# Moving two transposes of gate rows and two outputs in the hand-written order of a gated attention and feed-forward block

## The chip, the cores and the metric

The kernel runs on one core of a Trainium2 chip. The metric is the device time of one execution in microseconds (us); lower is better. TensorE does the matrix products and the transposes, VectorE (DVE in the rows) and ScalarE (ACT) read its results out of PSUM, GpSimd (POOL) does masks and a few elementwise operations, and SyncE (SP) issues all DMA transfers.

## The reference, cut to what matters

A batch of 16 sequences of 256 tokens, 512 wide, goes through two gated blocks:

```python
x = x + tanh(g_xattn[0]) * xattn(layernorm(x), ctx, ctx, ...)
x = x + tanh(g_ffn[0]) * ffn(layernorm(x), w_gate, w_up, w_down)
```

`xattn` has 8 heads of width 64. For each head two gates come from a product of the concatenated inputs with small matrices. With `cs` the running sum of `log_sigmoid(fg)` over the tokens and `a = ig - cs`, the decay matrix is `D = exp(cs_i + a_j - max_log_D_i)` for `j <= i`, so its row maximum is a running maximum of `a` along the tokens. The head is `(q k^T / 8 * D) / normaliser @ v`, followed by a root-mean-square norm of each head.

`ffn` quantises its input to 8 bits per token and its weights to {-1, 0, 1}. It computes `g = x @ w_gate.T` and `u = x @ w_up.T` (2048 wide), then `h = relu(g)**2 * u`, quantises `h` with the maximum of `|h|` in the token's row, and multiplies with `w_down.T` back to 512.

## The kernel before

The sequences are worked off one after another, each as two tiles `t = 0, 1` of 128 tokens. There are 16 steps. Step `b` (`par` is its parity) interleaves three sequences: the feed-forward block of `b`, the attention of `n = b + 1`, and the gates of `m = b + 2`. In the last two steps `m` is None, and in the last one `n` is None too. Each engine has its own list of work, written out by hand in a function `step`, and works it off strictly in order; semaphores join the lists. What an engine waits for therefore holds up all that stands behind it in its own list.

A feed-forward tile is four chunks of 512 hidden columns. `chunk(b, t, c)` on TensorE is four matmuls with the gate weights into the PSUM bank `gb[c % 2]` and four with the up weights into `ub[c % 2]` (L1090). ScalarE takes the relu of `gb` (L524) and squares it (L526). VectorE multiplies with `ub` in `hidden(b, t, c)` (L755); that product also frees the `ub` bank for chunk `c + 2`. `hidden_max` finds the row maximum in two parts: part 0 over three chunks (L762) and part 1 over the fourth (L767). `hidden_scale` (L777 to L782) makes the scale from it, and `quantise_low` on VectorE (L788) with `quantise_high` on ScalarE (L544) quantise half of the row each. `hidden_transposes` (L1104, 16 of them) turns the quantised rows, `hidden_cols` copies them out of PSUM (ScalarE L538, VectorE L796), `down` is 16 matmuls into the one bank `yb` (L1116), and `output(b, t)` on VectorE (L805) scales the bank, adds the residual and so frees it for the next `down`. SyncE stores the result.

The attention of `n`: `scores` (L1124, L1125) fills the banks `ab`, `weigh` on VectorE (L862) multiplies them with the decay matrix, which ScalarE's `exponentials` (L564, L570) and GpSimd's `masks` (L429) have made, and `heads_out` (L1137) multiplies with the values. Then `normaliser`, `head_squares`, `scale_heads` (L896, L900), `residual` (VectorE L908 for tile 0, GpSimd L436 for tile 1), `token_stats` (L915, L919), `token_centres`, `quantise_tokens`, `token_columns` (L1198).

The gates of `m`: `cumulative_sum` on TensorE (L1174, L1175), `cumulative` on VectorE (L842 copies the sums, L843 makes `a`), `a_rows` on TensorE (L1180, two transposes of `a`), `running_max` on VectorE (L848, a scan of these rows), `max_columns` on TensorE (L1187). SyncE's `spread_max` carries the rows through DRAM into the decay matrix.

All of the gates' small products share the PSUM bank `tp`, and the wait in front of `a_rows` is that `a` has been made:

```python
pe.wait_ge(tp_free, gate_use(m, CUMSUM) + 1)
```

GpSimd's `residual` waits for VectorE's last `output` as well (`gp.wait_ge(o_ready, 2 * n - 2)`), since `x2` of that parity is still being read by it.

Of the kernel before, what the change touches and what calls it, by code (L numbers as in the profile page):

```python
# [32 lines left out]
def gated_block(nc, x, ctx_t, ctx_v, small_in, w_gate, w_up, w_down, max_rows, out):  # L33
# [12 lines left out]
    KF = FF // P  # L46
# [7 lines left out]
    with ExitStack() as stack:  # L54
# [669 lines left out]
        def _(dve):  # L724
# [25 lines left out]
            def hidden(b, t, c):  # L750

                k = 8 * b + 4 * t + c
                dve.wait_ge(r2_ready, k + 1)
                dve.wait_ge(u_full, k + 1)
                nc.vector.tensor_tensor(h[t][:, c * CH:(c + 1) * CH], relu[:, c % 2, :], ub[c % 2][:, :],  # L755
                                        ALU.mult).then_inc(h_done, 1)
# [28 lines left out]
            def quantise_low(b, t):  # L785

                dve.wait_ge(quant_step, QUANT_K * (2 * b + t) + 5)
                nc.vector.tensor_scalar(hq[t][:, 0:FF // 2], h[t][:, 0:FF // 2], hqs[:, t:t + 1], MAGIC16,  # L788
                                        ALU.mult, ALU.add).then_inc(quant_step, 1)
# [9 lines left out]
            def output(b, t, xpar):  # L799
                k = 2 * b + t  # L800
                dve.wait_ge(y_full, k + 1)
                dve.wait_ge(dq_ready, k + 1)
                if not at(b, 0):
                    dve.wait_ge(out_done[t], 16 * b)
                nc.vector.scalar_tensor_tensor(ot[t][:, :], yb[:, :], dq[:, t:t + 1], x2[xpar][:, t, :],  # L805
                                               ALU.mult, ALU.add).then_inc(o_ready, 1)
# [32 lines left out]
            def cumulative(m, par):  # L839
                dve.wait_ge(tp_full, FULL * (gate_use(m, CUMSUM) + 1))  # L840
                cs = tp[:, 0:T * NH].rearrange("p (t g) -> p t g", t=T)
                nc.vector.tensor_copy(csum[:, :, :], cs).then_inc(gate_step, 1)  # L842
                nc.vector.tensor_tensor(a[par][:, :, :], gates[:, :, 0:NH], cs, ALU.subtract).then_inc(tp_free, 1)  # L843

            def running_max(m, par):

                dve.wait_ge(tp_full, FULL * (gate_use(m, A_ROWS) + 1))
                nc.vector.tensor_tensor_scan(mrow[:, :], tp[0:NH, 0:S], zeros8[:, :], LOWEST,  # L848
                                             ALU.max, ALU.add).then_inc(tp_free, 1)
# [44 lines left out]
            def scale_heads(n):  # L894
                dve.wait_ge(rms_step, 2 * n + 2)
                nc.vector.scalar_tensor_tensor(scl[:, :, :], rz[:, :, :], tanhs[:, 0:1], rn[:, :, :],  # L896
                                               ALU.mult, ALU.mult).then_inc(post_step, 1)
                dve.wait_ge(post_step, POST_K * n + 9)
                for t in range(T):
                    nc.vector.tensor_tensor(yo[:, t, :].rearrange("p (h d) -> p h d", d=HD), ysb[:, t, :, 0:HD],  # L900
                                            scl[:, t, :, None].to_broadcast([P, NH, HD]), ALU.mult).then_inc(post_step, 1)
# [89 lines left out]
            def step(b, n, m, par):  # L991
                npar = 1 - par
                prev = not at(b, 0)
                if n is not None:
                    weigh(n, 0)
                    weigh(n, 1)
                hidden(b, 0, 0)
                if m is not None:
                    attention_stats(m, par)
                if n is not None:  # L1000
                    weigh(n, 2)
                    weigh(n, 3)
                hidden(b, 0, 1)
                if n is not None:
                    weigh(n, 4)
                    weigh(n, 5)
                hidden(b, 0, 2)
                if n is not None:
                    weigh(n, 6)
                    weigh(n, 7)  # L1010
                if m is not None:
                    attention_norm(m, par)
                hidden_max(b, 0, 0)
                hidden(b, 0, 3)
                if prev:
                    hidden_cols(b - 1, 1)
                hidden_max(b, 0, 1)
                if n is not None:
                    normaliser(n, npar)
                if not prev:  # L1020
                    weight_scale(2)
                    dve.wait_ge(winv_step, WINV[2])
                    nc.vector.scalar_tensor_tensor(wprod[:, 2:3], wmean[:, 2:3], 1.0 / 127.0, tanhs[:, 1:2],
                                                   ALU.mult, ALU.mult).then_inc(winv_step, 1)
                hidden_scale(b, 0, par)
                quantise_low(b, 0)
                if n is not None:
                    head_squares(n)
                if m is not None:
                    gates_in(m)  # L1030
                if n is not None:
                    mean_squares(n)
                if m is not None:
                    log_forget(m)
                if n is not None:
                    scale_heads(n)
                if prev:
                    output(b - 1, 1, npar)
                if m is not None:
                    cumulative(m, par)  # L1040
                if n is not None:
                    residual(n, npar)
                if m is not None:
                    running_max(m, par)
                if n is not None:
                    token_stats(n, npar)
                hidden(b, 1, 0)
                if n is not None:
                    token_centres(n, npar)
                hidden(b, 1, 1)  # L1050
                if n is not None:
                    quantise_tokens(n)
                hidden_cols(b, 0)
                hidden(b, 1, 2)
                if m is not None:
                    negated_max(m)
                hidden_max(b, 1, 0)
                hidden(b, 1, 3)
                hidden_max(b, 1, 1)
                output(b, 0, par)  # L1060
                hidden_scale(b, 1, par)
                quantise_low(b, 1)

            schedule(dve, step)
            hidden_cols(LAST, 1)
# [4 lines left out]
        def _(pe):  # L1070
# [172 lines left out]
            def step(b, n, m, par):  # L1243
                npar = 1 - par
                prev = not at(b, 0)
                chunk(b, 0, 0, par)
                if n is not None:
                    scores(n, 0, npar)
                    scores(n, 1, npar)
                chunk(b, 0, 1, par)  # L1250
                if n is not None:
                    scores(n, 2, npar)
                    scores(n, 3, npar)
                    heads_out(n, 0, npar)
                chunk(b, 0, 2, par)
                if n is not None:
                    scores(n, 4, npar)
                    scores(n, 5, npar)
                    heads_out(n, 1, npar)
                    scores(n, 6, npar)  # L1260
                    scores(n, 7, npar)
                chunk(b, 0, 3, par)
                if n is not None:
                    heads_out(n, 2, npar)
                if prev:
                    hidden_transposes(b - 1, 1)
                else:
                    weight_total(2)
                if n is not None:
                    heads_out(n, 3, npar)  # L1270
                if m is not None:
                    q_columns(m, par)
                if prev:
                    down(b - 1, 1, 0, KF // 2)
                if m is not None:
                    gate_products(m, par, 0, 2 * T * KD)
                if prev:
                    down(b - 1, 1, KF // 2, KF)
                if m is not None:
                    cumulative_sum(m)  # L1280
                chunk(b, 1, 0, par, 0, 1)
                if m is not None:
                    a_rows(m, par)
                chunk(b, 1, 0, par, 1, 2)
                chunk(b, 1, 1, par)
                hidden_transposes(b, 0)
                chunk(b, 1, 2, par)
                if m is not None:
                    max_columns(m)
                down(b, 0, 0, KF // 2)  # L1290
                chunk(b, 1, 3, par)
                if n is not None:
                    token_columns(n)
                down(b, 0, KF // 2, KF)

            schedule(pe, step)
            hidden_transposes(LAST, 1)
# [34 lines left out]
```

## Time and profile before

| | |
|---|---|
| time, median of 3 runs | 637.5 us (636.77 to 637.85) |
| profiled execution, its own time | 638.38 us |
| profiled execution, span of the instructions | 636.7 us |
| TensorE matmul busy | 578.6 us, 91% of the span |
| VectorE busy | 526.7 us, 83% |
| ScalarE busy | 454.3 us, 71% |
| GpSimd busy | 129.9 us, 20% |
| mean granted TensorE clock | 0.965 |

The span runs from the first to the last instruction; the execution's own time lies 1.7 us above it. The first 100 us or so prepare the weights, and step 0 is mixed with that; from then on a step is repeated every 35.2 us. Timeline rows give the start in us from the start of the span, the time from the first start to the last end of the group, engine, source line and operation, what is written from what, and the number of instructions; a bracket is the idle time of the engine ahead of it and the instruction that is taken to have ended it.

### The profile page before, as it was taken

The page shows a single profiled execution, that of the slowest core. Times are in us where ns is not written, and L with a number is a line of the kernel's source. Part 1 is how long each engine was busy: PE and PEld are TensorE (multiplying, and loading weights), DVE is VectorE, ACT ScalarE, POOL GpSimd, SP SyncE. Part 2 cuts the span into 40 slices and gives each one's busy share as a digit, 9 for nine tenths or more (in the row PEclk, how much of TensorE's full clock was granted, in tenths as well). Part 3 has the DMA queues.
Part 4 walks back from the last instruction along what each step waited for, and adds up shares of the span by engine and source line. Part 5 has one row for each costly group of instructions (what it writes and reads, how often), then busy time and mean ns, then how long its engine had stood idle before and what let it go on. Part 6 is the DMA issues. An engine that isn't in the chain of part 4 may idle for free.

```text
span 636.7 us, 18420 instructions
## 1 busy us (share of the span) xinstructions
PE 578.6 (91%) x6596; PEld 338.0 (53%) x6596; DVE 526.7 (83%) x1144; ACT 454.3 (71%) x925; POOL 129.9 (20%) x266
## 2 busy tenths in 40 slices
PE   7592768999999999999999999999999999999896
PEld 4361443656555564656555565646565555656442
DVE  4479595898989989898989899898989899897964
ACT  5374979858685877858686868768586868677662
POOL 1256240212121202112121202021121212021200
PEclk9785968999999999999999999999999999999998
DMA  9884505041140505050320505050412305020000
GB/s 311 306 287 139 192 2 167 18 140 62 43 159 17 182 0 199 0 182 17 103 95 19 179 8 191 0 187 11 156 43 77 121 17 183 3 100 1 34 19 33
DMA packets 45169, 63.73 MB, mean 100 GB/s; under 512 B 1872, under 2 KB 26704, under 8 KB 45136
## 3 DMA queue, kind: packets, MB, share of 16 engines
q1 hardware_dynamic: 45136, 63.30, 28.8%
q8 instruction: 20, 0.33, 0.2%
q14 instruction: 13, 0.11, 0.1%
HBM read 54.77 MB, written 8.52 MB: 99 GB/s over the span
## 4 chain that ended last, share of the span: by engine, by line
PE 59%; DVE 17%; issue 10%; ACT 6%; DMA 5%; DVEq 1%; POOL 1%; SPq 0%; ACTq 0%; POOLq 0%
PE ub L1090 15%; PE gb L1090 14%; PE yb L1116 10%; PE ab L1124 6%; PE tp L1137 5%; PE ab L1104 3%; DVE ssq L883 3%; DMA stage<-in_w_up 2%; PE ab L1125 2%; DVE stage L805 2%; DMA xs<-in_x 2%; DVE stage L755 1%; DMA max_rows<-mrow 1%; PE ab L1198 1%; DVE dmat L862 1%
## 5 line engine op out<-in xcount | busy, mean ns | idle before, releaser
L1090 PE MATMUL ub<-wuT,xqT 128*128 128x512 bf16 x512 | 133.1, 383 | 2.0 <-DVE stage L755 2.0
L1090 PE MATMUL gb<-wgT,xqT 128*128 128x512 bf16 x512 | 133.3, 383 | 1.5 <-ACT xqT L551 1.5
L524 ACT ACTIVATE relu<-gb 128x512 f32<-128x512 f32 x128 | 75.4, 589 | 77.3 <-PE gb L1090 75.1
L1116 PE MATMUL yb<-wdT,stage 128*128 128x512 bf16 x512 | 122.8, 384 | 3.6 <-ACT stage L538 3.6
L755 DVE TENSOR_TENSOR stage<-relu,ub 128x512 f32<-128x512 f32 x128 | 87.0, 680 | 26.6 <-ACT relu L526 26.1
L862 DVE SCALAR_TENSOR_TENSOR dmat<-ab,dmat 128x384 f32<-128x384 f32 x128 | 65.3, 551 | 31.7 <-POOL dmat L429 22.7
L526 ACT ACTIVATE relu<-relu 128x512 f32<-128x512 f32 x128 | 80.7, 631 | 4.1
L1090 PEld LDWEIGHTS ub<-wuT,xqT 128*128 128x128 bf16 x512 | 50.3, 99 | 61.2 <-DVE stage L755 3.0
L1116 PEld LDWEIGHTS yb<-wdT,stage 128*128 128x128 bf16 x512 | 47.4, 99 | 53.4 <-issue 4.7
L1090 PEld LDWEIGHTS gb<-wgT,xqT 128*128 128x128 bf16 x512 | 46.0, 100 | 49.9 <-ACT xqT L551 1.8
L429 POOL TENSOR_SCALAR_AFFINE_SELECT dmat<-dmat 128x256 f32<-128x256 f32 x128 | 55.3, 461 | 68.0 <-ACT dmat L570 67.9
L1137 PE MATMUL tp<-values,dmat 128*64 128x65 f32 x1536 | 60.4, 229 | 3.6 <-issue 3.6
L1137 PEld LDWEIGHTS tp<-values,dmat 128*64 128x64 f32 x1536 | 51.5, 141 | 15.9 <-issue 10.8
L1124 PE MATMUL ab<-qT,cT 64*128 64x256 f32 x256 | 52.7, 437 | 5.4 <-DVE dmat L862 5.4
L570 ACT ACTIVATE dmat<-dmat,a 128x256 f32<-128x256 f32 x128 | 57.3, 496 | 0.0
L762 DVE TENSOR_REDUCE stage<-stage 128x1 f32<-128x1536 f32 x32 | 56.0, 1749 | 0.1
L459 POOL TENSOR_SCALAR dq<-hm,wprod 128x1 f32<-128x1 f32 x32 | 9.1, 284 | 222.8 <-DVE rhm L780 217.7
L564 ACT ACTIVATE dmat<-dmat,a 128x128 f32<-128x128 f32 x128 | 43.7, 391 | 7.0 <-DMA dmat<-max_rows 7.0
L436 POOL TENSOR_TENSOR x<-ysq,xs 128x512 f32<-128x512 f32 x16 | 28.4, 1774 | 82.4 <-DVE stage L805 78.3
L544 ACT ACTIVATE hq<-stage,hqs 128x1024 f16<-128x1024 f32 x32 | 36.7, 1146 | 5.7 <-DVE hqs L782 5.7
L578 ACT ACTIVATE ysb<-tp 128x260 f32<-128x260 f32 x64 | 24.5, 382 | 22.5 <-PE tp L1137 22.5
L1124 PEld LDWEIGHTS ab<-qT,cT 64*128 64x128 f32 x256 | 24.8, 188 | 26.5 <-issue 19.3
(110 smaller groups left out, 870.8 us busy)
## 6 DMA issues: line engine op xcount, KB each, us to landing
dmat<-max_rows SPq DMA_DIRECT2D x16, 1024.0 KB, 5.1
values<-in_ctx_v SPq DMA_DIRECT2D x16, 520.0 KB, 7.7
xs<-in_x SPq DMA_DIRECT2D x16, 512.0 KB, 5.9
cT<-in_ctx_t SPq DMA_DIRECT2D x16, 512.0 KB, 6.9
out<-stage SPq DMA_DIRECT2D x32, 256.0 KB, 2.0
stage<-in_w_gate SPq DMA_DIRECT2D x4, 1024.0 KB, 12.7
stage<-in_w_up SPq DMA_DIRECT2D x4, 1024.0 KB, 11.1
stage<-in_w_down SPq DMA_DIRECT2D x4, 1024.0 KB, 5.6
```

The lines of the kernel that those rows point to most:

```text
L429: nc.gpsimd.affine_select(out=dv, in_=dv, compare_op=ALU.is_ge, fill=0.0, base=0, pattern=[[0, 2], [1, P]], channel_multiplier=-1).then_in ...
L524: nc.scalar.activation(relu[:, c % 2, :], gb[c % 2][:, :], ACT.Relu).then_inc(g_free, 1)
L526: nc.scalar.activation(relu[:, c % 2, :], relu[:, c % 2, :], ACT.Square).then_inc(r2_ready, 1)
L564: nc.scalar.activation(dmat[:, hd, 2, :], dmat[:, hd, 1, :], ACT.Exp, bias=a[npar][:, 1, hd:hd + 1], scale=-1.0).then_inc(e_low, 1)
L570: last = nc.scalar.activation(dh, dh, ACT.Exp, bias=a[npar][:, 0, hd:hd + 1], scale=-1.0)
L755: nc.vector.tensor_tensor(h[t][:, c * CH:(c + 1) * CH], relu[:, c % 2, :], ub[c % 2][:, :], ALU.mult).then_inc(h_done, 1)
L762: nc.vector.tensor_reduce(h[t][:, FF:FF + 1], h[t][:, 0:3 * CH], axis=AX_X, op=ALU.max, apply_absolute_value=True).then_inc(quant_step, 1)
L862: nc.vector.scalar_tensor_tensor(dh, ab[hd % 2][:, 0:3 * P], HD ** -0.5, dh, ALU.mult, ALU.mult).then_inc(a_free[hd % 2], 1)
L1090: last = nc.tensor.matmul(bank[c % 2][:, :], xqT[par][:, t, d, :], w[:, d, c * CH:(c + 1) * CH], start=(d == 0), stop=(d == KD - 1))
L1116: done = nc.tensor.matmul(yb[:, :], hqT[:, c, :], wdT[:, c, :], start=(c == 0), stop=(c == KF - 1))
L1124: nc.tensor.matmul(ab[e][:, 0:S], cT[npar][rows, kd, 0:P], qT[npar][rows, kd, 0:S], start=True, stop=True)
L1137: done = nc.tensor.matmul(tp[rows, (2 * t + e) * VW:(2 * t + e + 1) * VW], dmat[:, hd, block, rows], values[npar][:, s, hd, :], start=firs ...
```

## The change

In every step that has an `m`, TensorE's `a_rows` goes from the middle of `chunk(b, 1, 0)` (between its gate half and its up half) to behind the whole chunk, and VectorE's `cumulative` goes ahead of `output(b - 1, 1)`. In the last two steps (no `m`), VectorE's `hidden(b, 1, 0)` goes ahead of `token_stats`. In the last step (no `n`), TensorE takes `chunk(b, 1, 3)` ahead of the whole of `down(b, 0)`, which was split around it, and VectorE's `output(b, 0)` goes behind `hidden_scale` and `quantise_low` of tile 1. No instruction is added or removed.

```diff
@@ VectorE, step
                     scale_heads(n)
+                if m is not None:
+                    cumulative(m, par)
                 if prev:
                     output(b - 1, 1, npar)
-                if m is not None:
-                    cumulative(m, par)
                 if n is not None:
                     residual(n, npar)
                 if m is not None:
                     running_max(m, par)
+                else:
+                    hidden(b, 1, 0)
                 if n is not None:
                     token_stats(n, npar)
-                hidden(b, 1, 0)
+                if m is not None:
+                    hidden(b, 1, 0)
...
                 hidden_max(b, 1, 1)
-                output(b, 0, par)
+                if n is not None:
+                    output(b, 0, par)
                 hidden_scale(b, 1, par)
                 quantise_low(b, 1)
+                if n is None:
+                    output(b, 0, par)
@@ TensorE, step
-                chunk(b, 1, 0, par, 0, 1)
+                chunk(b, 1, 0, par)
                 if m is not None:
                     a_rows(m, par)
-                chunk(b, 1, 0, par, 1, 2)
                 chunk(b, 1, 1, par)
                 hidden_transposes(b, 0)
                 chunk(b, 1, 2, par)
                 if m is not None:
                     max_columns(m)
-                down(b, 0, 0, KF // 2)
-                chunk(b, 1, 3, par)
-                if n is not None:
+                if n is not None:
+                    down(b, 0, 0, KF // 2)
+                    chunk(b, 1, 3, par)
                     token_columns(n)
-                down(b, 0, KF // 2, KF)
+                    down(b, 0, KF // 2, KF)
+                else:
+                    chunk(b, 1, 3, par)
+                    down(b, 0, 0, KF)
```

## Rows read from the trace of the kernel before

**Rows 1.** Busy time of each engine in one step, from the windows.

```profile
290.10:325.30 35.20, 34.18 (x409) 20.24 (x408) 31.14 (x71) 26.06 (x58) 6.62 (x15) 1.00 0.26 90
```

**Rows 2.** Waits of TensorE: total us, times, longest.

```profile
PE tp L1180 <- DVE a L843: 12.1, 14, 0.9
```

**Rows 3.** Timeline of TensorE in that step, where the gates' rows are transposed.

```profile
308.44 1.02 PE L1090 MATMUL gb<-wgT,xqT 128*128 128x512 bf16 x4
310.38 0.38 PE L1180 MATMUL tp<-ident,a 128*8 128x128 f32 x2 [0.92 <-DVE a L843]
...
314.94 1.03 PE L1090 MATMUL ub<-wuT,xqT 128*128 128x512 bf16 x4
```

**Rows 4.** Timeline of VectorE beside it.

```profile
309.42 0.75 DVE L805 SCALAR_TENSOR_TENSOR stage<-yb,dq,x 128x512 f32<-128x512 f32 x1
...
310.24 0.68 DVE L908 TENSOR_TENSOR x<-ysq,xs 128x512 f32<-128x512 f32 x1
310.84 0.67 DVE L848 TENSOR_TENSOR_SCAN mrow<-tp,zeros 8x256 f32<-8x256 f32 x1
...
313.04 0.69 DVE L755 TENSOR_TENSOR stage<-relu,ub 128x512 f32<-128x512 f32 x1
```

**Rows 5.** Timeline of GpSimd's residual, in that step and two before the end.

```profile
310.25 1.81 POOL L436 TENSOR_TENSOR x<-ysq,xs 128x512 f32<-128x512 f32 x1 [5.54 <-DVE stage L805]
...
590.91 0.68 DVE L908 TENSOR_TENSOR x<-ysq,xs 128x512 f32<-128x512 f32 x1
...
591.15 1.57 POOL L436 TENSOR_TENSOR x<-ysq,xs 128x512 f32<-128x512 f32 x1 [5.37 <-DVE stage L805]
```

**Rows 6.** Timeline of TensorE and VectorE in the next step, scores and weighing.

```profile
324.11 0.40 PE L1125 MATMUL ab<-qT,cT 64*128 64x128 f32 x4
...
324.62 1.02 DVE L862 SCALAR_TENSOR_TENSOR dmat<-ab,dmat 128x384 f32<-128x384 f32 x2 [0.32 <-POOL dmat L429]
...
327.13 0.92 PE L1137 MATMUL tp<-values,dmat 128*64 128x65 f32 x24
...
330.85 1.02 DVE L862 SCALAR_TENSOR_TENSOR dmat<-ab,dmat 128x384 f32<-128x384 f32 x2 [1.53 <-POOL dmat L429]
...
332.78 1.04 PE L1090 MATMUL gb<-wgT,xqT 128*128 128x512 bf16 x4
```

**Rows 7.** Timeline of the last step but one (b = 14), TensorE and ScalarE.

```profile
594.25 1.01 ACT L538 ACTIVATE stage<-ab 128x1024 bf16<-128x1024 f16 x1
...
594.45 1.04 PE L1090 MATMUL ub<-wuT,xqT 128*128 128x512 bf16 x4 [1.82 <-DVE stage L755]
595.40 1.89 PE L1116 MATMUL yb<-wdT,stage 128*128 128x512 bf16 x8
```

**Rows 8.** Timeline of the last step (b = 15), TensorE.

```profile
619.33 1.89 PE L1116 MATMUL yb<-wdT,stage 128*128 128x512 bf16 x8
...
626.89 1.71 PE L1104 MATMUL ab<-identh,hq 128*128 128x128 f16 x16 [2.22 <-DVE hq L788]
629.02 4.35 PE L1116 MATMUL yb<-wdT,stage 128*128 128x512 bf16 x16 [0.41 <-ACT stage L538]
```

**Rows 9.** Timeline of the last step, VectorE.

```profile
620.68 1.75 DVE L762 TENSOR_REDUCE stage<-stage 128x1 f32<-128x1536 f32 x1
623.41 0.69 DVE L755 TENSOR_TENSOR stage<-relu,ub 128x512 f32<-128x512 f32 x1 [0.98 <-ACT relu L526]
624.14 0.69 DVE L767 TENSOR_REDUCE hmax<-stage 128x1 f32<-128x513 f32 x1
...
625.40 0.20 DVE L777 TENSOR_SCALAR hm<-hmax,c 128x1 f32<-128x1 f32 x1
```

**Rows 10.** Timeline of TensorE's same work earlier in the last step.

```profile
607.93 1.06 PE L1104 MATMUL ab<-identh,hq 128*128 128x128 f16 x16
609.81 3.61 PE L1116 MATMUL yb<-wdT,stage 128*128 128x512 bf16 x16 [0.82 <-ACT stage L538]
```

**Rows 11.** Window of TensorE near the end: busy us, granted clock, DMA share, GB/s.

```profile
626.80:628.80 2.00, 1.71 (x16) 0.58 0.12 44
```

## The prediction

> **What bounds the kernel now.** I first read the windows of one step, to see which engine has no room. In 35.2 us TensorE is busy for 34.18, VectorE for 31.14, ScalarE for 26.06 and GpSimd for 6.62 [rows 1]. So a step costs what TensorE's list costs, plus its own waits. The waits of TensorE come next: one kind repeats, `a_rows` waiting for `a` from VectorE, 12.1 us in 14 waits of at most 0.9 [rows 2]. The timeline shows its place. TensorE starts the gate half of `chunk(b, 1, 0)` at 308.44 and stands for 0.92 us until 310.38 [rows 3]. VectorE is then in `output(b - 1, 1)`, at 309.42; the two small instructions of `cumulative` sit between it and `residual` at 310.24 [rows 4]. Behind the wait stand four up matmuls that need nothing of it. The last view was the timeline of the last two steps, where no `a_rows` exists, and where the end of the kernel is a chain through VectorE and not TensorE's work [rows 8, 9].
>
> **Part 1: `a_rows` behind the chunk, `cumulative` ahead of the output.** A group of four matmuls takes 0.86 us of TensorE's time: 16 take 3.61 and 8 take 1.89, so eight more cost 1.72 [rows 8, 10]. With both halves of the chunk ahead of it, TensorE comes to `a_rows` at 308.44 + 2 x 0.86 = 310.16, some 0.1 later with the change of operands. `cumulative` now starts where the output did, at 309.42, and its two instructions are short: rows that follow each other on VectorE overlap by some 0.08 (310.24 + 0.68 against 310.84), so the output takes 0.67 of the 0.82 us up to `residual`, and the two together 0.15. So `a` is there by about 309.7. There is 0.5 us to spare and the wait goes. The whole of it is TensorE's time: everything behind starts 0.92 earlier.
>
> What VectorE gives for it: `output` comes 0.16 later and `residual` still starts at 310.24. `running_max` starts at 310.84 [rows 4]; the transposes, started at about 310.26 and 0.38 long [rows 3], end at 310.64, a little earlier than now. So the scan, SyncE's transfer of the rows behind it and `max_columns` stay where they are. The output frees `yb` for `down(b, 0)` four groups later, and its store is not waited for here. Both are free.
>
> GpSimd's residual waits for that output. It starts at 310.25 and ends at 312.06; in step 14 it takes 1.57 and not 1.81, and in both cases it ends 1.13 or 1.14 us behind the end of VectorE's own residual (310.92; 591.59 against 592.72) [rows 4, 5]. I take from this that its end hangs on VectorE's residual, which does not move: 0 us. The other bound is that it slips by the output's 0.16. That pushes `token_stats` and `hidden(b, 1, 0)` by as much, and it is this product that frees the bank for the up half of chunk 2: it ends at 313.73, TensorE will want it at 314.94 - 0.92 = 314.02 [rows 3, 4]. Even 0.16 later it is in time. The Trainium skill, SBUF — State Buffer, section "Who interferes with whom", says that a VectorE instruction with two SBUF inputs and a GpSimd instruction that reads SBUF exclude each other for the length of an instruction; by it the slip is 0, by the start of the output alone it would be 0.16 a step, and neither changes the time of TensorE here by more than 0.1 a step.
>
> **Is there room for a shorter step in the other engines?** TensorE now leads VectorE by 0.92 more from `a_rows` until VectorE next waits for it. VectorE idles in the next step for 1.53 and 0.32 in front of `weigh` [rows 6]. The critical hand-off is `weigh(1)`: the scores of heads 2 and 3 need its bank. The pattern is seen at `weigh(4)`, `weigh(5)`, which end at 331.87 while the chunk behind the next pair of scores starts at 332.78, so 0.91 later [rows 6]. `weigh(1)` ends at 325.64, so `heads_out(0)` can't start before 326.55, and TensorE wants it at 327.13 - 0.92 = 326.21 [rows 6]. If `weigh(0)` stays at 324.62, 0.34 of each 0.92 is lost. Its row names GpSimd's mask for the 0.32 idle, but the last scores of heads 0 and 1 start at 324.11 and end at 324.51, just ahead of it, and these come 0.92 earlier. The same releaser is named at 330.85, behind a mask that belongs to a later pair. So I hold it for a wait on TensorE: `weigh(0)` moves up by 0.32 to 324.30, `weigh(1)` ends at 325.32, and the bound on `heads_out(0)` is 326.23 against the wanted 326.21. The two loops are as good as equal, and I take the full gain; the bounds are 0.58 and 0.92 a step.
>
> The wait is counted 14 times, but in step 0, with the weights still being made, it is next to nothing, and 13 steps carry it at 0.92: **12.0 us**. The bounds are 13 x 0.58 = 7.5 and 13 x 0.98 = 12.7 (if 0.06 of the hand-off goes too).
>
> **Part 2: the product ahead of the token statistics.** In step 14 TensorE waits 1.82 us for `hidden(14, 1, 0)` in front of the up half of chunk 2, at 594.45 [rows 7]. With the product some 2 us earlier this wait goes, but what is behind it is `down`, at 595.40. It needs ScalarE's copy, which starts at 594.25 and ends at 595.26 [rows 7]; the one in the last step ends 0.15 ahead of its `down` too. In front of this copy ScalarE's list has the logarithm for the token statistics, and these wait for GpSimd's residual, until 592.72 [rows 5], whatever stands ahead of them. So the stall only moves from the up half to `down`, as a pause of 1.82 + 0.2 = about 2.0: **0 us**. Its other bound is the whole 1.82 of gain, if the copy is early, which its order on ScalarE excludes. VectorE is 0.6 us (one product) further on; TensorE has no wait on it until the end, so this too is 0. In the last step the edit moves nothing, since there `token_stats` is absent.
>
> **Part 3: the last step.** Now eight matmuls of `down` start at 619.33, ahead of chunk 3 [rows 8]. They go behind, so chunk 3 comes 1.72 earlier and its product is no longer late: it is bound by the large maximum in front of it, 620.68 + 1.67 = 622.35, and not by 623.41 [rows 9]. That is 1.06. Behind it stand the small maximum at 624.14 and, after the output, the scale at 625.40 [rows 9]. Without the output the scale can start when the maximum is done, 624.14 + 0.69 + 0.07 = 624.90, which gives 0.50. The sum is **1.56 us** on the chain to the last transposes at 626.89. The 16 matmuls of `down(15, 0)` end about 619.33 + 1.72 + 3.45 = 624.5, ahead of the transposes at 625.33. The output, moved behind the quantiser, ends about 626.0; the last `down` needs it and the transposes' copy, which is there at 627.3. So it is covered by 1.3 us. Bounds: 1.06 and 1.72 + 0.66 = 2.38.
>
> **The clock.** At 626.89, after TensorE had stood 2.22 us, the transposes take 1.71 and run at a granted clock of 0.58, with parts at 1.2 GHz; the last `down` takes 4.35 [rows 8, 11]. The same two groups at 607.93 and 609.81 take 1.06 and 3.61, behind pauses of at most 0.82 [rows 10]. From the first transpose to `down` it is 2.13 us now and was 1.88 there. At the full clock the tail is shorter by 0.25 + 0.74 = 0.99. The pause ahead of the transposes shrinks from 2.22 to about 0.8, the size of the one that did no harm, so I take **0.99 us**; bounds 0 and 0.99.
>
> **The sum.** 12.0 + 0 + 1.56 + 0.99 = 14.6 us. Against the profiled execution's own time of 638.38 (a span of 636.7 with 1.7 around it) this gives 623.8. The median of the runs, 637.5, is 0.9 lower, and whether it has the slow clock at its end is not known. Taken from it, the time would be 622.9. I forecast **623.0 us**. The likeliest case's own range is 621.8 to 624.6.
>
> **Rivals.**
> (A) VectorE's loop becomes the bound: `weigh(0)` really waits for GpSimd's mask, or the hand-off is tighter than read. Then a step gains 0.58: 7.5 + 2.6 = 10.1, and 627.4 us. For it speaks the releaser in the row; against it the end of the scores just ahead.
> (B) The clock falls elsewhere. In step 14 the pause grows to 2.0, between 1.82 (no fall) and 2.22 (a fall) [rows 7, 8]. A low stretch costs, by the two groups above, up to 0.65 + 0.74 = 1.4 us: 624.4. With the last clock low as well, 625.4.
> (C) The wait only moves: after `a_rows` comes earlier relative to VectorE, TensorE meets a later wait of the same size in each step, and only the end gains, 2.6: 634.9. For it speaks VectorE's 31.14 busy of 35.2; against it, that its idle time ahead of `weigh` alone is 1.85 a step, twice the gain.
> (D) Slower. The rows reach the scan late. VectorE stands in front of `running_max` and all of its list behind is late, up to `weigh` of the next step. There are 0.2 us of room before it starts. To undo the 0.92 and the end's 2.6 the rows must come about 0.2 + 0.34 + 0.92 = 1.5 us later than I have them; at 2 us later, 13 x 0.5 - 2.6 gives about 641 us. The rows' timeline leaves no such lateness.
>
> **How the numbers follow.** The sum as it stands 0.73, A 0.12, B 0.08, C 0.04, D 0.03. A measurement here can tell about 0.2%, 1.3 us. All cases but D are faster than that, and something for what I have not thought of goes to the same and the slower side: faster 0.94, same 0.02, slower 0.04. The range reaches from all upper bounds together, 637.5 - 12.7 - 2.38 - 0.99 = 621.4, up to A: 621.5 to 627.5.
>
> **What the profile of the changed kernel would show.** In every step, `a_rows` without idle time in front and `running_max` in its old place behind VectorE's residual; steps 34.3 us apart; `hidden(b, 1, 0)` ending just ahead of the up half of chunk 2; VectorE's idle time in front of `weigh` down to some 0.6 in place of 1.53, and none at `weigh(0)`. In step 14, no wait at the up half but about 2.0 at `down`, on ScalarE's copy. In the last step, a pause of about 0.8 ahead of the transposes, which take 1.06, and a last `down` of 3.61. The forecast is wrong if TensorE waits in front of the scores of heads 2 and 3 or of chunk 2 in each step, or if the steps stay above 34.7 us.

## The result and the profile after

The changed kernel takes 620.49 us (median of 4, 619.63 to 621.43) against 637.15 us for the kernel before (median of 4 runs on the same chip). The ratio is 0.9738, with a 95% interval from 0.972 to 0.9755: 2.6% faster. The forecast was 623.0 with a range from 621.5 to 627.5, so the sign was right and the gain, 16.7 us where the sum had 14.6, was larger than the range allowed. The profiled execution has a span of 619.7 us, where it was 636.7: 17.0 us less.

The timeline of TensorE in the changed kernel, at the place that answers to [rows 3]:

```profile
302.56 1.02 PE L1096 MATMUL gb<-wgT,xqT 128*128 128x512 bf16 x4
303.42 1.03 PE L1096 MATMUL ub<-wuT,xqT 128*128 128x512 bf16 x4
304.28 0.38 PE L1186 MATMUL tp<-ident,a 128*8 128x128 f32 x2
304.50 1.03 PE L1096 MATMUL gb<-wgT,xqT 128*128 128x512 bf16 x4
```

No bracket stands in front of the rows (L1186). The distance from start to start tells more: from the gate half of chunk 0 to that of chunk 1 it is 304.50 - 302.56 = 1.94 us. Before, the gate half started at 308.44 and the rows at 310.38 [rows 3]; the rows hold TensorE for 0.22 and the up half for 0.86, so the next chunk began 3.02 behind the first:

```profile
310.60 1.03 PE L1090 MATMUL ub<-wuT,xqT 128*128 128x512 bf16 x4
311.46 1.03 PE L1090 MATMUL gb<-wgT,xqT 128*128 128x512 bf16 x4
```

The difference is 1.08 us, and not the 0.92 of the bracket. The rows of VectorE that answer to [rows 4, 5], and GpSimd's:

```profile
303.54 0.17 DVE L842 COPY csum<-tp 128x16 f32<-128x16 f32 x1
303.63 0.16 DVE L843 TENSOR_TENSOR a<-gates,tp 128x16 f32<-128x16 f32 x1
303.70 0.74 DVE L805 SCALAR_TENSOR_TENSOR stage<-yb,dq,x 128x512 f32<-128x512 f32 x1
304.37 0.68 DVE L908 TENSOR_TENSOR x<-ysq,xs 128x512 f32<-128x512 f32 x1
304.97 0.67 DVE L848 TENSOR_TENSOR_SCAN mrow<-tp,zeros 8x256 f32<-8x256 f32 x1
...
304.53 1.65 POOL L436 TENSOR_TENSOR x<-ysq,xs 128x512 f32<-128x512 f32 x1 [5.70 <-DVE stage L805]
...
318.21 1.00 DVE L862 SCALAR_TENSOR_TENSOR dmat<-ab,dmat 128x384 f32<-128x384 f32 x2
...
323.90 1.02 DVE L862 SCALAR_TENSOR_TENSOR dmat<-ab,dmat 128x384 f32<-128x384 f32 x2 [1.00 <-POOL dmat L429]
```

The scan stands where it did, 0.60 behind the start of VectorE's residual. GpSimd's residual starts 0.15 later after VectorE's than it did, and is shorter by as much: it ends at 306.18, which is 1.13 behind the end of VectorE's own (305.05); in the two rows of before it was 1.14 and 1.13. `weigh(0)` at 318.21 has no idle time in front of it any more.

The last two steps, TensorE, answering to [rows 7, 8]:

```profile
578.08 1.03 PE L1096 MATMUL ub<-wuT,xqT 128*128 128x512 bf16 x4
581.03 1.89 PE L1122 MATMUL yb<-wdT,stage 128*128 128x512 bf16 x8 [1.92 <-ACT stage L538]
...
606.90 3.40 PE L1122 MATMUL yb<-wdT,stage 128*128 128x512 bf16 x15
610.92 1.07 PE L1110 MATMUL ab<-identh,hq 128*128 128x128 f16 x16 [0.62 <-DVE hq L788]
612.80 3.61 PE L1122 MATMUL yb<-wdT,stage 128*128 128x512 bf16 x16 [0.82 <-ACT stage L538]
```

The wait of step 14 is now in front of `down`, as forecast. In the last step the pause ahead of the transposes is 0.62, they take 1.07 and the last `down` 3.61, at the full clock.

**Where the 17.0 us came from.** I set the start of the rows in each step against that of before. In steps 3 to 13 the distance from one step to the next fell from 35.22 to 34.16, 1.06 each, 11.7 us in 11 steps. Step 2 fell from 35.95 to 34.18: 1.06 again, and 0.7 us that only the kernel before had, a pause in the middle of its gate products. Steps 0 and 1 together have 0.9, mixed with what the preparation of the weights shifted (this allows for the up half that now stands ahead of the rows), step 14 has nothing, and the last step gives 2.6. In sum 11.7 + 1.8 + 0.9 + 2.6 = 17.0.

### The profile page after: what moved, and what is told of

Its sections match the earlier page's. It is cut to its first block, busy times and chain, and to the rows that moved or that the text cites. A ratio compares the mean times of both kernels' runs of the same rounds, so it can differ in the third digit from the quotient of the medians.

```text
span 619.7 us, 18325 instructions
## 1 busy us (share of the span) xinstructions
PE 565.0 (91%) x6517; PEld 337.9 (55%) x6596; DVE 524.0 (85%) x1144; ACT 454.4 (73%) x925; POOL 127.9 (21%) x266
## 4 chain that ended last, share of the span: by engine, by line
PE 75%; ACT 7%; DVE 7%; DMA 5%; issue 5%; SPq 1%; POOL 0%; DVEq 0%; ACTq 0%
PE yb L1122 17%; PE gb L1096 16%; PE ub L1096 16%; PE tp L1143 7%; PE ab L1130 6%; PE ab L1110 4%; PE tp L1170 3%; DMA stage<-in_w_up 2%; PE ab L1153 2%; PE ab L1131 2%; DMA max_rows<-mrow 2%; PE ab L1204 1%; DMA xs<-in_x 1%; ACT wdT L516 1%; ACT wdT L506 1%
## 5 line engine op out<-in xcount | busy, mean ns | idle before, releaser
L1096 PE MATMUL gb<-wgT,xqT 128*128 128x512 bf16 x480 | 128.1, 385 | 6.0 <-issue 4.0
L1096 PE MATMUL ub<-wuT,xqT 128*128 128x512 bf16 x498 | 130.2, 383 | 0.8
L1122 PE MATMUL yb<-wdT,stage 128*128 128x512 bf16 x482 | 114.3, 379 | 8.0 <-ACT stage L538 4.9
L436 POOL TENSOR_TENSOR x<-ysq,xs 128x512 f32<-128x512 f32 x16 | 26.3, 1644 | 83.7 <-DVE stage L805 79.6
L1130 PEld LDWEIGHTS ab<-qT,cT 64*128 64x128 f32 x256 | 25.3, 190 | 25.7 <-issue 16.7
```

The source lines that it names most:

```text
L1096: last = nc.tensor.matmul(bank[c % 2][:, :], xqT[par][:, t, d, :], w[:, d, c * CH:(c + 1) * CH], start=(d == 0), stop=(d == KD - 1))
L1122: done = nc.tensor.matmul(yb[:, :], hqT[:, c, :], wdT[:, c, :], start=(c == 0), stop=(c == KF - 1))
L1130: nc.tensor.matmul(ab[e][:, 0:S], cT[npar][rows, kd, 0:P], qT[npar][rows, kd, 0:S], start=True, stop=True)
```

## The experiments

Theory S: the bracket shows less than the wait costs. It is counted from the modelled end of the last matmul (309.46), while the next one could have begun at 308.44 + 0.86 = 309.30 [rows 3]. Theory B: the bracket is all of it, and the rest of the gain came from elsewhere. The first four runs shared a chip; the kernel before took 636.84 there (13 runs).

**Part 1 alone (e1).** Only the two moves for the rows, as in the diff of the change.

```diff
+                if m is not None:
+                    cumulative(m, par)
                 if prev:
                     output(b - 1, 1, npar)
-                if m is not None:
-                    cumulative(m, par)
...
-                chunk(b, 1, 0, par, 0, 1)
+                chunk(b, 1, 0, par)
                 if m is not None:
                     a_rows(m, par)
-                chunk(b, 1, 0, par, 1, 2)
```

> Part 1 alone (rows behind the chunk, cumulative ahead of the output). Theory S: the wait in front of the rows was worth 1.08 us of TensorE's time a step, not the 0.92 that stood in the bracket, because the matmul ahead of it gives its place free 0.16 before its modelled end. Then 13 steps give 13.8 to 14.0 and the time is 623.2 (622.5 if the 0.7 in step 2 goes as well). Theory B: the bracket was the whole wait, and the rest of the gain of 2 us came from elsewhere, a code fetch or the clock: 12.0, so 625.2.

Measured: 623.27 us, ratio 0.9783 (0.9746 to 0.982), steps 34.14 to 34.19 us apart. S holds: it is the steps that tell, since a gain from elsewhere would not stand in each of them, and they are 1.06 us shorter than the 35.22 of before. Its last `down`, still in the old order, takes 5.03 us.

**Part 3 alone (e2).** Only the order of the last step.

```diff
-                down(b, 0, 0, KF // 2)
-                chunk(b, 1, 3, par)
-                if n is not None:
+                if n is not None:
+                    down(b, 0, 0, KF // 2)
+                    chunk(b, 1, 3, par)
                     token_columns(n)
-                down(b, 0, KF // 2, KF)
+                    down(b, 0, KF // 2, KF)
+                else:
+                    chunk(b, 1, 3, par)
+                    down(b, 0, 0, KF)
...
-                output(b, 0, par)
+                if n is not None:
+                    output(b, 0, par)
                 hidden_scale(b, 1, par)
                 quantise_low(b, 1)
+                if n is None:
+                    output(b, 0, par)
```

> Part 3 alone, only the last step's order. Both theories: 1.56 us less chain on VectorE, and with no low clock at the end 0.99 more, so 634.6; without the clock's share 635.6. Theory S has no say on step 2: if the 0.7 us in the gate products of step 2 are a code fetch that depends on where the step falls in time, they are still there, as in the kernel before.

Measured: 634.74 us, ratio 0.996 (0.9943 to 0.9976), steps 35.22 apart, the last `down` at 3.61 us. Its size is as expected. The pause of the kernel before in step 2 is absent here (168.58 - 133.36 = 35.22), though the steps are those of the kernel before, so it is not the change that takes it away.

**Rows moved, sums not (e3).** TensorE's edit alone.

```diff
-                chunk(b, 1, 0, par, 0, 1)
+                chunk(b, 1, 0, par)
                 if m is not None:
                     a_rows(m, par)
-                chunk(b, 1, 0, par, 1, 2)
```

> Only a_rows behind the whole chunk, cumulative still behind the output. The result a is ready at the same moment as in the kernel before, 310.32, and TensorE's place is free at 310.17, while the modelled end of the matmuls is 310.33. Theory S: 0.21 us are still lost a step although the trace will show a bracket of 0.05 or none; gain 0.86 a step, 626.0, that is 2.6 more than with both halves. Theory B: with no idle time in the bracket nothing is lost, so within 0.6 us of the run with both halves.

Measured: 627.95 us, ratio 0.9853 (0.9818 to 0.9887), 4.7 us more than with both halves (e1), steps 34.36 apart. This is the run that decides. Its timeline of TensorE:

```profile
304.21 1.02 PE L1090 MATMUL gb<-wgT,xqT 128*128 128x512 bf16 x4
305.07 1.03 PE L1090 MATMUL ub<-wuT,xqT 128*128 128x512 bf16 x4
306.16 0.38 PE L1180 MATMUL tp<-ident,a 128*8 128x128 f32 x2
306.38 1.03 PE L1090 MATMUL gb<-wgT,xqT 128*128 128x512 bf16 x4
```

No bracket, and yet the next chunk starts 2.17 us behind the first and not 1.94. The 0.23 us are lost with no bracket in TensorE's list: the rows begin 1.09 behind the up half, where 0.86 is enough. That they wait for `a` stands in the rows of the weight load (PEld), which takes `a` into TensorE ahead of the transpose:

```profile
305.94 0.16 DVE L843 TENSOR_TENSOR a<-gates,tp 128x16 f32<-128x16 f32 x1
306.15 0.09 PEld L1180 LDWEIGHTS tp<-ident,a 128*8 128x8 f32 x2 [0.56 <-DVE a L843]
```

`a` is done at 306.10, the load begins at 306.15 and the transposes at 306.16, which is only 0.06 behind the modelled end of the up half (305.07 + 1.03). From step to step it is 34.36 against 34.16, so of the 4.7 us 13 x 0.20 = 2.6 is this. The rest is not in the steps. The profile of e3 has the pause in step 2 again (0.7 us), which e1's has not, and its last `down` takes 6.48 us at half the clock, 1.45 more than e1's.

```profile
615.79 1.10 PE L1104 MATMUL ab<-identh,hq 128*128 128x128 f16 x16 [2.22 <-DVE hq L788]
617.67 6.48 PE L1116 MATMUL yb<-wdT,stage 128*128 128x512 bf16 x16 [0.78 <-ACT stage L538]
```

```profile
616.70:623.50 6.80, 6.02 (x17) 0.50 0.00 0
```

The second fence is the window of TensorE over that stretch: the granted clock is 0.50.

**Sums moved, rows not (e4).** VectorE's edit alone.

```diff
+                if m is not None:
+                    cumulative(m, par)
                 if prev:
                     output(b - 1, 1, npar)
-                if m is not None:
-                    cumulative(m, par)
```

> Only cumulative ahead of the output, a_rows still between the halves of the chunk. The result a is ready at 309.66, 0.66 earlier than before. Both theories: the bracket falls from 0.92 to 0.26 and each step gains 0.66, so 628.6. If the position of the rows in TensorE's list were the cause alone, there would be no gain: 637.2.

Measured: 630.03 us, ratio 0.9882 (0.9847 to 0.9917), steps 34.57 apart, so 0.65 a step. The bracket reads as expected. Set against the changed kernel it speaks for S too: the bracket is 0.26, but the rows begin 1.29 behind the gate half, where 0.86 is enough, and the steps are 0.41 longer than 34.16. The profile shows one thing that can account for the 1.4 us over the expectation: its last `down` takes 6.47 us, where the kernel before had 4.35.

```profile
304.61 1.02 PE L1090 MATMUL gb<-wgT,xqT 128*128 128x512 bf16 x4
305.90 0.38 PE L1180 MATMUL tp<-ident,a 128*8 128x128 f32 x2 [0.26 <-DVE a L843]
```

**Part 2 alone (e5).** The next four runs shared a chip as well; the kernel before took 637.15 there.

```diff
                 if m is not None:
                     running_max(m, par)
+                else:
+                    hidden(b, 1, 0)
                 if n is not None:
                     token_stats(n, npar)
-                hidden(b, 1, 0)
+                if m is not None:
+                    hidden(b, 1, 0)
```

> Part 2 alone, the product ahead of the token statistics in the last two steps, in the kernel before. My theory: the 1.82 us of wait in step 14 only move from the up half of chunk 2 to the down product behind it, which waits for ScalarE's copy: about 2.0 there, gain 0, so the time of the kernel before. Rival: the wait was VectorE's and is gained, 1.8 us.

Measured: 637.71 us, ratio 1.0007 (0.9991 to 1.0023). By the medians the three parts alone take 13.6, 2.1 and -0.6 us off, 15.1 in sum, and the whole change 16.7; e1's interval alone is 2.3 us wide to either side, so no interaction of the parts can be read from that. The wait stands in front of `down`:

```profile
595.67 1.89 PE L1119 MATMUL yb<-wdT,stage 128*128 128x512 bf16 x8 [1.91 <-ACT stage L538]
```

This run also has the old order at its end, and there the clock did not fall, although the pause is the same 2.22 us as before:

```profile
627.16 1.07 PE L1107 MATMUL ab<-identh,hq 128*128 128x128 f16 x16 [2.22 <-DVE hq L788]
629.05 3.61 PE L1119 MATMUL yb<-wdT,stage 128*128 128x512 bf16 x16 [0.82 <-ACT stage L538]
```

**ScalarE's copy first (e6).** Made on the changed kernel; `hidden(b, 1, 0)` also goes ahead of `token_stats` in every step.

```diff
-                if n is not None:
-                    tokens_rstd(n)
                 hidden_cols(b, 0)
+                if n is not None:
+                    tokens_rstd(n)
```

> The changed kernel, with ScalarE's copy for the down product ahead of its logarithm for the token statistics, and the product ahead of the statistics, both in every step. If the stall of 1.92 us in step 14 is the order on ScalarE, it goes; TensorE then meets VectorE's quantised tokens, and 0.85 us remain as gain: 619.6. In the other steps TensorE's list is full, so nothing changes there: steps stay at 34.16. Rival: VectorE's chain sets step 14 anyway, no gain.

Measured: 620.19 us, ratio 0.9736 (0.9711 to 0.9761) to the kernel before; steps 34.14 apart. Step 14:

```profile
577.62 1.03 PE L1093 MATMUL ub<-wuT,xqT 128*128 128x512 bf16 x4
578.48 1.89 PE L1119 MATMUL yb<-wdT,stage 128*128 128x512 bf16 x8
...
581.56 1.04 PE L1093 MATMUL ub<-wuT,xqT 128*128 128x512 bf16 x4 [0.32 <-DVE stage L755]
582.78 0.40 PE L1201 MATMUL ab<-identh,xq 128*128 128x128 f16 x4 [0.19 <-DVE xq L945]
583.47 0.38 PE L1201 MATMUL ab<-identh,xq 128*128 128x128 f16 x4 [0.29 <-DVE stage L796]
```

The stall was the order on ScalarE: its copy (L538) now starts at 576.57, ahead of the logarithm at 578.99. From the up half of chunk 2 to the first matmuls of step 15 it is 7.80 us here (577.62 to 585.42) and 8.57 in the changed kernel (578.08 to 586.65): 0.77 gained, 0.85 expected. The times of the runs can't tell these two kernels apart.

**Scores between the halves of a chunk (e7), and with e6 (e8).** In the changed kernel the scores of heads 6 and 7 hold TensorE for 1.26 us where the other pairs take 0.86, with no bracket.

```diff
                     heads_out(n, 1, npar)
-                    scores(n, 6, npar)
-                    scores(n, 7, npar)
-                chunk(b, 0, 3, par)
+                chunk(b, 0, 3, par, 0, 1)
+                if n is not None:
+                    scores(n, 6, npar)
+                    scores(n, 7, npar)
+                chunk(b, 0, 3, par, 1, 2)
```

> The changed kernel, with the scores of heads 6 and 7 between the halves of chunk(b, 0, 3). Now the pair takes 1.26 us of TensorE's time where the others take 0.86, since head 7 waits for its bank; that 0.40 a step stands in no bracket. Theory T (TensorE's list alone sets the step): 0.40 gained in 14 steps, 614.9. Theory V (VectorE's loop over weigh and the quantiser is as long as TensorE's list): weigh(6) now comes 0.2 later and everything behind it on VectorE, the bank of chunk (b, 1, 2) comes late, and the step gets 0.14 to 0.16 longer: 622.5.

> The last two edits together. Theory T: 614.0. Theory V: the product ahead of the statistics takes the wait at the bank away, but the loop over weigh(1), heads_out(0) and ScalarE is still 0.16 longer: 621.7, steps of about 34.3.

Measured: 627.56 us, ratio 0.9842 (0.9811 to 0.9872), steps 34.55; and 625.08 us, 0.9808 (0.978 to 0.9836), steps 34.54. Theory T falls, though the edit does what it is for: the chunk and the two scores together take 2.80 us of TensorE's time in e7 (328.05 to 330.85) where they take 3.09 in the changed kernel (324.56 to 327.65). That is 0.29 less, and not 0.40, since the scores begin 0.97 behind the gate half and not 0.86. V had the direction, but neither the size nor the place, which both traces show at the second four q transposes; this is e7's:

```profile
333.55 0.66 PE L1153 MATMUL ab<-ident,q 128*128 128x128 f32 x4
335.00 0.63 PE L1153 MATMUL ab<-ident,q 128*128 128x128 f32 x4 [0.79 <-DVE stage L796]
```

VectorE shows where the lateness begins. Here are `weigh(4)` and `weigh(6)` in e7, and then in the changed kernel:

```profile
327.38 1.02 DVE L862 SCALAR_TENSOR_TENSOR dmat<-ab,dmat 128x384 f32<-128x384 f32 x2 [0.99 <-POOL dmat L429]
...
330.06 1.02 DVE L862 SCALAR_TENSOR_TENSOR dmat<-ab,dmat 128x384 f32<-128x384 f32 x2 [0.30 <-PE ab L1131]
```

```profile
323.90 1.02 DVE L862 SCALAR_TENSOR_TENSOR dmat<-ab,dmat 128x384 f32<-128x384 f32 x2 [1.00 <-POOL dmat L429]
...
326.19 1.01 DVE L862 SCALAR_TENSOR_TENSOR dmat<-ab,dmat 128x384 f32<-128x384 f32 x2
```

In e7 `weigh(6)` waits for the scores, which now stand behind the gate half, and starts 2.68 us behind `weigh(4)` and not 2.29. These 0.39 us are what a step is longer (34.55 against 34.16).

The changed kernel waits at the same q transposes, without a bracket, and I had not seen it. These are VectorE's copy there and the two groups of four transposes:

```profile
330.30 0.68 DVE L796 TENSOR_SCALAR stage<-ab 128x1024 bf16<-128x1024 f16 x1
...
330.35 0.66 PE L1153 MATMUL ab<-ident,q 128*128 128x128 f32 x4
...
331.12 0.63 PE L1153 MATMUL ab<-ident,q 128*128 128x128 f32 x4
```

Transposes of a group start 0.11 us apart at its end (the fourth at 330.73), but the fifth starts 0.39 behind the fourth, at 331.12, 0.14 after the copy has ended; in e7 it starts 0.15 after it (334.85, 335.00). So 0.28 us a step are spent waiting for VectorE there, again ended just behind the modelled end of the last matmul (331.11) and so not shown as idle, in the kernel before as well (fourth at 337.69, copy done at 337.93, fifth at 338.08). In e7 the same distance is 1.07, a wait of 0.96: 0.68 more, which is the 0.39 that `weigh(6)` comes later and the 0.29 that TensorE comes earlier.

**The loop shortened (e9, e10).** Both are made on e8. VectorE's copy goes earlier in both:

```diff
+                if prev:
+                    hidden_cols(b - 1, 1)
                 hidden(b, 0, 3)
-                if prev:
-                    hidden_cols(b - 1, 1)
```

In e9 alone, the first two heads of the next step are also weighed ahead of the quantiser:

```diff
                     weigh(n, 1)
+                if prev:
+                    quantise_low(b - 1, 1)
                 hidden(b, 0, 0)
...
                 hidden_scale(b, 1, par)
-                quantise_low(b, 1)
                 if n is None:
+                    quantise_low(b, 1)
                     output(b, 0, par)
```

> The last kernel (both edits), and on VectorE also the copy of the transposed rows ahead of hidden(b, 0, 3), and the scores of heads 0 and 1 weighed ahead of quantise_low of the previous tile. The two runs before showed the 0.8 us wait of a step in front of the second four q transposes, for VectorE's copy; that copy now comes 0.6 earlier, and weigh(1) some 0.6 too. If the loop through VectorE was what made those kernels slow, TensorE's list sets the step again, now without the 0.40 at head 7: steps of 33.9 to 34.0 and 617.0. If the scores' place itself costs TensorE time, steps stay at 34.5 and the time at 625.

> As the one before, without the weighing ahead of the quantiser: only the copy comes earlier. The wait in front of the q transposes falls from 0.8 to 0.2, but the loop weigh(1), heads_out(0), ScalarE, hidden(b, 0, 2), weigh(6) has only 0.14 of room: steps of 34.4, 623.1. If that loop has more room than I read, the steps fall to 33.95 as in the run beside it, 617.

The kernel before took 637.85 beside these. Measured: 626.87 us, ratio 0.9826 (0.9806 to 0.9846), steps 34.58; and 626.0 us, 0.9818 (0.9795 to 0.984), steps about 34.62. Both expectations missed in what they took for likely. e9's other case, that the scores' place itself costs TensorE time, has the number (34.5), but the traces don't bear it out: at that place TensorE takes 0.29 us less, and what it loses it loses in waits for VectorE. The wait in front of the q transposes fell to 0.20 as I had it, and another came up 6 us further on, in front of the cumulative sum; e9's:

```profile
334.64 0.63 PE L1152 MATMUL ab<-ident,q 128*128 128x128 f32 x4 [0.20 <-DVE stage L796]
...
340.43 0.39 PE L1179 MATMUL tp<-logf,upper 128*128 128x16 f32 x2 [0.40 <-DVE logf L836]
```

So it isn't the loop over `weigh(1)` and `heads_out(0)`: e9 shortened that one and gained nothing over e10. The traces point to the stretch of VectorE's list from `weigh(6)` to `log_forget`. In all four runs `weigh(6)` starts when the scores of heads 6 and 7 are done (0.30 or 0.31 us of waiting for them), VectorE then works for some 10 us with one idle time, of 0.22, and TensorE waits for what it takes from that stretch: for the copy in e7 and e8, for the copy and `logf` in e9 and e10. No run shortens this stretch by itself, so it is read from the traces and not shown by an experiment. Nor was the earlier copy tried on the changed kernel, where up to 0.28 us a step could be had by it (an estimate, from the wait of 0.28 there).

**The changed kernel again (e11).**

> The changed kernel once more, beside the others on the same chip: 620.5, steps of 34.16. It tells whether the 0.7 us in the gate products of step 2 are absent again, and whether the clock stays up in the last step: with no pause of over 0.82 us there, it should.

Measured: 620.95 us, ratio 0.9742 (0.9724 to 0.9761); steps 34.14 to 34.20, no pause in step 2, and the clock stays up in the last step. No version ran clearly ahead of it.

## Why the prediction was right in kind and short in size

**What bounds the kernel:** right. TensorE's list, with one repeated wait that a bracket shows. A second one of 0.28 a step, for VectorE's copy at the q transposes, stands in no bracket; it is the same before and after, so it is no part of the gain. Steps of 34.3 were forecast, and 34.16 measured.

**Part 1: this step failed, in the size of its main term.** It says "the whole of it is TensorE's time: everything behind starts 0.92 earlier", with 0.98 a step as the upper bound. The measured value is 1.06 to 1.08, so 13.8 us and not 12.0, which lies outside the bound of 12.7. The numbers for the right value stood one line above it, in the prediction's own text: a group of four takes 0.86, so TensorE was free for the rows at 309.30 and took them at 310.38. I took the bracket of the row instead and called the difference a hand-off. I had also charged 0.1 for the change of operands, and there is none: the rows start exactly 0.86 behind the up half. e3 and e4 show that this is how the idle time is counted and no side effect of the order. Each step costs 1.06 with a bracket of 0.92, 0.41 with one of 0.26 (e4) and 0.20 with none (e3); the difference is the 0.16 by which the modelled end of four matmuls (1.02) lies behind the place where the next ones can begin (0.86).

**The one-off in step 2**, 0.7 us, was not in the sum. It is a pause of 0.56 inside the gate products of the kernel before. The profiles of e3 and e10 have it too (0.54, 0.52) and, shorter, those of e4, e5, e8 and e9 (0.25 to 0.28); it is absent in the changed kernel twice and in e1, e2, e6 and e7. So it comes and goes with and without each part of the change, and what makes it is open. With it and the 1.8 us of part 1 the profile's 17.0 us stand against a sum of 14.6.

**GpSimd's residual:** right, 0. Its start moved by 0.15 and its end did not, 1.13 us behind VectorE's. The Trainium skill, SBUF — State Buffer, section "Who interferes with whom", calls the port pair that VectorE shares with GpSimd an exclusive lock, so that of two such instructions the later one waits for the whole of the first. The trace agrees: it takes 1.65 us where it was 1.81, in step with the later start.

**Room in the other engines:** right. `weigh(0)` waited for TensorE's scores and not for the mask that the row names; it moved up and no wait came up at the scores of heads 2 and 3. Against the gate half of `chunk(b, 1, 0)` it starts 0.53 earlier (15.65 behind it, 16.18 before), while GpSimd's masks start only 0.14 earlier (14.77 and 14.91). The forecast had 0.32. By its own reckoning of the hand-off (the end of `weigh(1)` plus 0.91) that would have held up `heads_out(0)` by 0.2 of the 1.08 us, and only the 0.53, which it did not foresee, leaves it free: it starts 17.61 behind the gate half, where it was 18.69. My figure for the idle time that would be left in front of `weigh(4)`, 0.6, was wrong: it is 1.00. It was 1.53, loses 1.06 to the shorter step, and VectorE gets there 0.5 us earlier in its own list, which I left out.

**Part 2:** right, 0. The stall moved to `down` (1.92 against some 2.0 forecast), and e6 shows the reason that was given, the order on ScalarE.

**Part 3 and the clock:** 2.6 measured in the profile, 2.55 forecast, and 2.1 by the medians of e2. The order's share is borne out: the pause ahead of the transposes fell from 2.22 to 0.62, so 1.60 where 1.56 was forecast. The clock's share is less certain than I wrote, and that the sum fits is in part luck, since it was taken from one profile of the kernel before. With the old order at the end, behind the same pause of 2.22 us, the last `down` took 3.61 us (e5), 4.35 [rows 8], 5.03 (e1), 6.47 (e4) and 6.48 (e3). So the saving depends on the execution and is between 0 and 2.9 us, where my bounds were 0 and 0.99. With the new order, and a pause of 0.62, it took 3.61 in all eight profiles (the changed kernel, e2, e6 to e11).

**The rivals:** A (VectorE's loop) did not come about here, but e7 to e10 show how near it is: a reordering that saves 0.29 a step of TensorE's own work made the step 0.4 longer. B: the pause of 1.92 in step 14 was followed by no fall of the clock. C and D did not occur.

**The range** failed because its lower end was put together from bounds of which the largest was built on the same bracket: with 13.8 in place of 12.7 it would have been 620.3, and the 620.49 would lie inside.

## What to carry to other kernels

Price a wait on TensorE from start to start, with and without the waiting group, by the spacing of the matmuls; the idle time that a row shows is less than what the wait costs, here by some 0.15 us each, and a wait of 0.2 us stood in no bracket of TensorE's list at all. The row of the weight load can still name it. Before moving a producer later to fill a gap on the engine that is the bottleneck, follow the consumer's list to the next thing the bottleneck takes from it: here that list had no slack over some 10 us, and closing a gap of 0.4 us made each step 0.4 us longer. A pause of two microseconds on TensorE near the end should be closed even when it looks covered: behind the one of 2.22 us here the clock fell in four profiles of five, and behind the one of 0.62 in none of eight.

## What the runs showed of the hardware that was not expected

The same pause of 2.22 us on TensorE, with the same work around it, was followed by a granted clock of 1.00 throughout in one profile (e5) and by a stretch at 0.50 in four others (before, e1, e3, e4), in which the same 16 matmuls took 4.35 to 6.48 us and not 3.61. The fall came at different places: in the kernel before some 0.2 us after the transposes had begun, in e3 and e4 near their end, 0.9 us after they had begun, and in e1 1.4 us after, when they were done.

This is the window of e1 over such a stretch, at 1.2 GHz:

```profile
613.20:616.60 3.40, 2.87 (x7) 0.50 0.00 0
```

In step 14, pauses of 1.91 us (e5, e11), 1.92 (the changed kernel) and 2.12 (e7) were not followed by a fall. The length of the pause alone doesn't decide it, then, and what else does is not shown here.
